# Two attention layers on one core: the first layer's head loop reordered, its value parts split in bulk, its low parts divided between VectorE and GpSimd

## What is computed

```python
text = ctx[:, :77]; ip = ctx[:, 77:]
q = split_heads(x @ Wq.T)
out_text = softmax(q @ k(text).T * 0.25) @ v(text)
out_ip   = softmax(q @ k_ip(ip).T * 0.25) @ v_ip(ip)
x = (out_text + out_ip) @ Wo.T + bo + x
```

## Time and profile before

| | |
|---|---|
| median of 3 runs | 1808.93 us (1806.72 to 1810.32) |
| the profiled execution's own time | 1810.82 us |
| its span | 1809.0 us |
| TensorE busy (matmul) | 1635.4 us, 90% |
| TensorE weight loads | 1234.2 us, 68% |
| VectorE busy | 1272.7 us, 70% |
| ScalarE busy | 1116.1 us, 62% |
| GpSimd busy | 463.6 us, 26% |
| mean granted clock | 0.96 |

### The profile page before, as it was taken

The page is one execution under the profiler, slowest core; times in us unless marked ns, Lnnn a source line. Parts: engine busy times, 40 slices in busy tenths (PEclk is TensorE's granted clock), DMA queues, the critical chain, the costliest instruction groups (busy, mean ns, idle before and its releaser), DMA issues.

```text
span 1809.0 us, 34075 instructions
## 1 busy us (share of the span) xinstructions
PE 1635.4 (90%) x8608; PEld 1234.2 (68%) x8608; DVE 1272.7 (70%) x3548; ACT 1116.1 (62%) x2323; POOL 463.6 (26%) x1225
## 2 busy tenths in 40 slices
PE   5788989999978898999988888999998889999993
PEld 2455469999445447999835544999974554799991
DVE  2487358887678717888758853788875883588875
ACT  1599157776279627777429943677734991577760
POOL 0244013232025302323104411222301540233220
PEclk9899989999989998999989999999998999899996
DMA  7210220000301031001030111100012102100000
GB/s 234 75 35 22 88 65 21 19 18 20 114 29 35 13 104 53 22 17 32 1 121 31 35 48 61 59 20 17 28 45 85 35 26 79 36 18 21 17 20 15
DMA packets 47284, 83.04 MB, mean 46 GB/s; under 512 B 4417, under 2 KB 11857, under 8 KB 47185
## 3 DMA queue, kind: packets, MB, share of 16 engines
q1 hardware_dynamic: 43040, 74.15, 12.5%
q10 hardware_dynamic: 4144, 7.76, 1.4%
HBM read 47.78 MB, written 34.10 MB: 45 GB/s over the span
## 4 chain that ended last, share of the span: by engine, by line
PE 77%; ACT 10%; issue 5%; DVE 5%; DMA 1%; POOL 1%; ACTq 1%; SPq 0%; POOLq 0%; DVEq 0%
PE ps_w L838 37%; PE ps_s L838 17%; PE ps_t L838 16%; PE ps_b L838 4%; ACT probsT_high L461 4%; ACT probsT L469 4%; DVE row_max L648 2%; PE ps_m L838 2%; ACT q_slot L454 1%; ACT probs L495 1%; POOL probsT_low L383 1%; ACT probs L478 0%; ACT probs L536 0%; DMA w_ki<-in_wki 0%; DVE row_max L679 0%
## 5 line engine op out<-in xcount | busy, mean ns | idle before, releaser
L637 DVE TENSOR_TENSOR probsT_low<-probsT,probsT_high 128x512 fp32r<-128x512 f32 x560 | 394.1, 704 | 85.2 <-ACT probsT L469 76.0
L461 ACT ACTIVATE probsT_high<-ps_t 128x512 fp32r<-128x512 f32 x640 | 382.6, 598 | 113.9 <-PE ps_t L838 109.9
L838 PE MATMUL ps_w<-gram,probsT_high 128*128 128x416 f32 (+2 forms) x1280 | 390.8, 316 | 0.0
L469 ACT ACTIVATE probsT<-ps_t 128x512 f32<-128x512 f32 x640 | 384.0, 600 | 0.0
L838 PE MATMUL ps_w<-gram_low,probsT_high 128*128 128x384 f32 (+2 forms) x1280 | 354.5, 305 | 0.0
L495 ACT ACTIVATE probs<-ps_s,exp_bias 128x508 f32<-128x508 f32 x320 | 220.9, 691 | 125.9 <-POOL exp_bias L394 82.6
L838 PE MATMUL ps_s<-k_slot,q_slot 96*128 96x512 f32 x640 | 249.6, 434 | 32.0 <-issue 13.0
L838 PE MATMUL ps_t<-q_slot,k_slot 98*128 98x512 f32 x640 | 266.1, 435 | 11.0 <-ACT q_slot L454 9.2
L394 POOL TENSOR_SCALAR exp_bias<-row_max 128x1 f32<-128x1 f32 x320 | 129.7, 405 | 551.8 <-DVE row_max L679 551.8
L838 PEld LDWEIGHTS ps_w<-gram_low,probsT_high 128*128 128x128 f32 (+1 forms) x1280 | 244.8, 191 | 11.1
L838 PEld LDWEIGHTS ps_w<-gram,probsT_high 128*128 128x128 f32 (+1 forms) x1280 | 243.2, 190 | 11.5
(11 more groups left out here) (153 smaller groups left out, 2056.9 us busy)
## 6 DMA issues: line engine op xcount, KB each, us to landing
q_slot<-parts_q SPq DMA_DIRECT2D x160, 96.0 KB
k_slot<-parts_k SPq DMA_DIRECT2D x160, 96.0 KB
parts_k<-probsT_high SPq DMA_DIRECT2D x24, 512.0 KB, 4.2
parts_q<-probsT_low SPq DMA_DIRECT2D x24, 512.0 KB, 4.3
parts_k<-probsT_high SPq DMA_DIRECT2D x24, 128.0 KB, 3.8
parts_q<-probsT_low SPq DMA_DIRECT2D x24, 128.0 KB, 3.6
ctx_sb<-in_ctxT ACTq DMA_DIRECT2D x3, 1024.0 KB, 8.3
vip_rep<-vip_rows SPq DMA_DIRECT2D x16, 160.0 KB, 3.6
```

The lines of the kernel that those rows point to most:

```text
L461: nc.scalar.activation(probsT_high[1 - par][:, t, :], ps_t[:, t % 2, :], ACT.Exp, scale=SCALE)
L469: nc.scalar.activation(probsT[:, t, :], ps_t[:, t % 2, :], ACT.Exp, scale=SCALE).then_inc(pt_block[l], 1)
L637: nc.vector.tensor_tensor(probsT_low[1 - par][:, t, :], probsT[:, t, :], probsT_high[1 - par][:, t, :].bitcast(F32), ALU.subtract).then_in ...
L838: return nc.tensor.matmul(out, lhsT, rhs, start=start, stop=stop)
```

## The change

In the first layer's head loop:
- **Order.** Scores are made three heads ahead instead of two (`AHEAD = 3`), through a loop of its own (`run_heads0`, 24 steps instead of 22). TensorE's order in a step is new; the transposed scores 0 of a head are the last work of the step before. The transposes of the outputs, their sum on VectorE and with it `out_all` come one step later.
- **Low parts.** Blocks 0 and 2 on GpSimd, 1 and 3 on VectorE, block 3 one step later.
- **Values.** Instead of four GpSimd operations per head that split the values, ScalarE writes the high parts and VectorE the low parts of all heads at once (`v0_high`, `v0_lows`), and GpSimd only copies both into the slot (two copies). The banks of these products are now freed by VectorE. `v0_lows` stands in the closing piece, behind the last of four groups of products.
- **Memory.** `v0_sb` becomes `v0_text` and `v0_ip`; `sz_all`, `fused`, `ip_sq`, `ip_norm2`, `rip` become parts of `out_all`; `ident` becomes `ident_r`.

```diff
 NEXT = (
     [("k0", m, "D") for m in range(CBN)]
     + [("q0", m, "D") for m in range(CBN)]
-    + [("v0t", 0, "A")]
-    + [("v0i", t, "A") for t in range(TB)]
+    + [("v0t", 0, "D")]
+    + [("v0i", t, "D") for t in range(TB)]
 )
...
+        def run_heads0(step, eng, b):
+            for n in range(-AHEAD, 1):
+                step(b, n, n % SLOTS, n // SLOTS, False, n >= 0, n >= -1, n >= -2, True)
+            with eng.Fori(0, TURNS - 1) as turn:
+                for n in range(1, SLOTS + 1):
+                    step(b, SLOTS * turn + n, n % SLOTS, turn + n // SLOTS, True, True, True, True, True)
+            for n in range(HEADS - AHEAD, HEADS + 1):
+                step(b, n, n % SLOTS, n // SLOTS, True, n < HEADS, n + 1 < HEADS, n + 2 < HEADS, False)
...
             # gpsimd
+                def low(t):
+                    pool.wait_ge(pt_block[0], TB * (g + 1) + t + 1 + CREDIT1)
+                    pool.sem_inc(passed, 1)
+                    nc.gpsimd.tensor_tensor(probsT_low[1 - par][:, t, :], probsT[:, t, :],
+                                            probsT_high[1 - par][:, t, :].bitcast(F32), ALU.subtract).then_inc(low_pool, 1)
+                if transposed:
+                    pool.wait_ge(oT_moved, g + CREDIT)
+                    pool.sem_inc(passed, 1)
+                    by_part = v0_slot[1 - par][:, :, :].rearrange("p t (g w) -> p t g w", w=V0H)
+                    nc.gpsimd.tensor_copy(by_part[:, :, 0:2, 0:D], v0_ip[:, :, n + 1, :, :])
+                    nc.gpsimd.tensor_copy(by_part[:, 0, 2:4, 0:D], v0_text[:, n + 1, :, :]).then_inc(v0_in, 1)
+                    low(0)
+                    low(2)
...
             # scalar
                 if transposed:
                     expT(b, 0, n, par, 0)
                     expT(b, 0, n, par, 1)
+                    expT(b, 0, n, par, 2)
+                if shifted:
+                    shift(b, 0, n + 1, k + 1)
+                if transposed:
+                    expT(b, 0, n, par, 3)
                 if use:
                     act.wait_ge(oT_done, HEADS * b + n + 1)
                     nc.scalar.activation(outT0[par], ps_w[par][0:V0S, :], ACT.Copy).then_inc(oT_moved, 1)
-                if transposed:
-                    expT(b, 0, n, par, 2)
-                if scores:
-                    shift(b, 0, n + 1, k + 1)
-                if transposed:
-                    expT(b, 0, n, par, 3)
...
             # vector
-            nc.vector.memset(v0_sb[:, :, :, :], 0.0)
...
+            def v0_lows(b):
+                before = 0 if b is FIRST else (1 + TB) * (b + 1)
+                def by_head(name, t, k):
+                    wait_job(dve, b, name, t)
+                    dve.wait_ge(v0_high_in, before + k + 1)
+                    return bank(name, t)[:, 0:C].rearrange("p (h d) -> p h d", d=D)
+                nc.vector.tensor_tensor(v0_text[0:TEXT0, :, 0, :], by_head("v0t", 0, 0)[0:TEXT0, :, :],
+                                        v0_text[0:TEXT0, :, 1, :].bitcast(F32), ALU.subtract).then_inc(freed["D"], 1)
+                for t in range(TB):
+                    nc.vector.scalar_tensor_tensor(out=v0_ip[:, t, :, 0, :], in0=by_head("v0i", t, 1 + t),
+                                                   scalar=ip_rows[:, 0:1] if t == 0 else 1.0,
+                                                   in1=v0_ip[:, t, :, 1, :].bitcast(F32),
+                                                   op0=ALU.mult, op1=ALU.subtract).then_inc(freed["D"], 1)
...
-                if scores:
-                    maxima(0)
-                if transposed:
-                    lowT(b, 0, n, par, 0)
-                if scores:
-                    maxima(1)
-                if transposed:
-                    lowT(b, 0, n, par, 1)
+                if use:
+                    lowT(b, 0, n - 1, 1 - par, 3)
+                if shifted:
+                    maxima(g + 2, row_max[0][par], 1)
+                if before:
+                    dve.wait_ge(o_done, g)
...
+                if transposed:
+                    lowT(b, 0, n, par, 1)
                 if scores:
+                    maxima(g + AHEAD, row_max[0][1 - par], 0)
...
                     if ahead and i < 2:
                         for m in ((0,), (1, 2))[i]:
                             low(b, "q0", m)
+                    if ahead and i == 3:
+                        v0_lows(b)
                     link(b, last)
...
             # tensor
+                if transposed:
+                    scoresT_of(0, g, k, 1)
+                if use:
+                    pe.wait_ge(oT_moved, g - 1 + CREDIT)
+                    pe.wait_ge(v0_in, g + 1)
+                    for t in range(TB):
+                        values_high(t)
+                if before:
...
+                    last.then_inc(o_done, 1)
+                if transposed:
+                    scoresT_of(0, g, k, 2)
+                if use:
+                    values_low(0)
+                    values_low(1)
+                if shifted:
+                    pe.wait_ge(max_half, 2 * (g + 3) + CREDIT)
+                    head_maxT(0, par)
+                if scores:
+                    scores_half(0)
+                if use:
+                    values_low(2)
+                    values_low(3).then_inc(oT_done, 1)
+                if transposed:
+                    scoresT_of(0, g, k, 3)
+                if scores:
+                    scores_half(1)
+                if shifted:
+                    scoresT_of(0, g + 1, k + 1, 0)
```

More of the change, by code:

```diff
@@ L572, in batch @@
                     highs(b, "q0")
[L573 to L575 removed]
+                    v0_high(b)
                 move_transposed(b, "tr1")
@@ L582, in _ @@
             highs(FIRST, "q0")
-            v0_text(FIRST)
-            for t in range(TB):
-                v0_ip(FIRST, t)
+            v0_high(FIRST)
             run_batches(act, batch)
@@ L638, in lowT, with step0, maxima @@
                                         ALU.subtract).then_inc(low_block[l], 1)
-            def step0(b, n, k, turn, use, transposed, scores):
+            def step0(b, n, k, turn, before, use, transposed, shifted, scores):
                 par = k % 2
-                def maxima(half):
+                g = HEADS * b + n
+                def maxima(j, rows, half):
                     cs = slice(2 * half, 2 * half + 2)
-                    dve.wait_ge(s_half, 2 * (HEADS * b + n + 2) + half + 1)
-                    nc.vector.tensor_reduce(out=row_max[0][par][:, cs, 0:1], in_=ps_s[:, :, 0:TEXT0], axis=AX.X, op=ALU.max)
-                    nc.vector.tensor_reduce(out=row_max[0][par][:, cs, SHIFT_ROWS - 1:SHIFT_ROWS], in_=ps_s[:, :, TEXT0:T],
+                    dve.wait_ge(s_half, 2 * j + half + 1)
+                    nc.vector.tensor_reduce(out=rows[:, cs, 0:1], in_=ps_s[:, :, 0:TEXT0], axis=AX.X, op=ALU.max)
+                    nc.vector.tensor_reduce(out=rows[:, cs, SHIFT_ROWS - 1:SHIFT_ROWS], in_=ps_s[:, :, TEXT0:T],
```

166 lines of the change are left out of this document (60 added, 106 removed).

## The result

The changed kernel takes **1821.57 us** (median of 5 runs, 1816.8 to 1822.75), the kernel before 1808.93 in the same comparison. The ratio is 1.0067, with a 95% interval of 1.0054 to 1.0081: slower by two thirds of a per cent. The profiled execution took 1822.75 with a span of 1820.9, 11.9 more than the span before (1809.0).

What follows compares the result with a forecast made beforehand. The prediction saw the first layer's head loop as a closed circle of waits, 5.46 us per head. Terms -9.8 (head stages), +10.6 (bulk split), +7.5 (clock), -0.8 (start) sum to +7.5: 1808.93 becomes 1816 us, range 1798 to 1825.

Steps and rivals of the forecast that it cites:

- The closing pieces: Last products to transposes: bulk value passes on VectorE delay the transposes by 3.55 us in three preparations, +10.6 us.
- The clock behind them: Output projections: TensorE's idle time drops its clock, costing 2.5 of a 3.05 us difference, three times, +7.5 us.
- rival 2: Closing pieces: the clock doesn't fall, as the last product splits the idle time; 1809 us, no change; chance 0.17.
- The first exponential: Fill of each head stage: transposed scores 0 of head 0 wait behind head 1's second score half, 2.45 us later.
- The steady head: First layer's head loop: the circle closes at 5.23 us instead of 5.46, 0.23 less per head, 3.9 for 17.
- I take 1.0 off: Fill of each stage: first two head spacings, no longer tied to the old circle, save 1.0 us (bounds 0 and 1.6).
- rival 3: Fill of each stage: low clock lasts one more head, 1.7 us times four, 6.8, giving 1823 us; chance 0.10.
- Rival 1: Head loop: VectorE and GpSimd don't hold each other up; ScalarE bounds heads at 5.06, about 1805 us; chance 0.20.
- the two readings: VectorE's lengthened subtraction: it stood still until GpSimd was done (chosen, head 5.23), or overlap costs a fixed 0.13 (5.11).
- the rule quoted in the prediction: VectorE instructions with two SBUF inputs and GpSimd instructions reading SBUF exclude each other for the whole instruction.
- 0.07 left over: Probability kept for what the prediction didn't see, split evenly; half was added to "faster", given as 0.27.
- The start's -0.8: Start of the kernel: VectorE's memset of 640 columns replaces one of 1600, so first loads wait 0.8 us less.

Runs made afterwards that it cites:

- e1: Changed kernel with the closing piece's five value-splitting passes spread: two behind the third product, one behind the fourth, two behind the last sum; 1803.92 us, ratio 0.9985.
- e2: Changed kernel with four unused matmuls added on TensorE ahead of the closing transposes in three preparations; 1812.69 us, ratio 1.0032.
- e3: Changed kernel without GpSimd's counting instruction between its wait for a block of exponentials and its subtraction; 1808.43 us, ratio 1.0023.
- e4: Changed kernel with GpSimd's block 0 subtraction replaced by four zero fills, so that low part is left out of the result; 1809.78 us, ratio 1.0017.
- e6: Changed kernel with an unused matmul ahead of each wait on a maximum while a stage's pipeline fills; 1811.18 us, ratio 1.0013.
- e7: Changed kernel with value passes spread, GpSimd's counting instruction removed, and VectorE's half 0 maximum and TensorE's first score half moved earlier; 1791.12 us, ratio 0.9910.
- e9: Changed kernel with spread value passes, no GpSimd counting instruction, earlier maximum and first score half, plus unused matmuls in the fill; 1789.67 us, ratio 0.9886.
- e5: Changed kernel with VectorE's half 0 maximum ahead of block 1's subtraction and TensorE's first score half directly behind transposed scores 2; 1804.93 us, ratio 0.9987.
- e8: Changed kernel with block 0's low part back on VectorE and GpSimd keeping block 2 alone; 1809.28 us, ratio 1.0016.

## Why the prediction was right or wrong

- **The closing pieces** were right in mechanism and size: 5.50 to 5.66 against 1.92, forecast +3.55 each. e1 and e2 show that the order of the passes makes it.
- **The clock behind them** was right: 2.8 instead of 2.5 each. Its price was read from the earlier trace rows as if that stretch were all at the low clock; in the trace the granted clock is 0.50 until 1798.68 and 1.00 after it, so the 3.05 are the price of 7.45 us at the low clock. The changed kernel's projections have 6.8 us of it, which is why the figure fitted. The prediction set rival 2 (no fall) at 0.17. In the changed kernel's profile all three fell, but e3 and e4 show that rival 2 isn't wrong in kind (below).
- **The first exponential** comes 9.82 after the first scores, before 7.37: the forecast 2.45.
- **The steady head failed by half.** The step was "GpSimd takes block 0 at once, as it does now". In the kernel before, GpSimd takes block 3 with a wait and the subtraction alone; block 0 is now taken in a helper with a counting instruction between. It starts 0.18 after the exponential, not 0.07, and as VectorE's end follows GpSimd's, the 0.11 passes into the circle: 5.36 instead of 5.23. e3 took the instruction out and got most heads back to 5.26. The prediction read "at once" from a row and didn't ask whether the new code issues the same instructions. Per head the gain was 0.13 (5.49 to 5.36, the loop's turns included), not 0.23, so 6.9 us of the forecast gain are missing over 68 heads.
- **"I take 1.0 off" in the fill failed**: nothing in the trace showed it, and it was not there. Taking 2.2 for the heads and 2.45 for the first exponential from the stage's +0.1 leaves -0.2. The first spacing between heads grew from 6.59 to 7.21 in the mean, since the clock stays low longer (in batch 2 until 18.6 us after the first scores, before until 14.3): rival 3, in part. e6 shows that the waits in the fill cost 1.2 per stage through it.
- **Rival 1 was priced wrong.** It gave a head of 5.06 if VectorE and GpSimd didn't touch each other. e4 took GpSimd's work away from beside VectorE's and got 5.24 to 5.27, since TensorE's own row closes at 5.24. Had rival 1 come true, the time would have been within 3 us of the forecast (5.24 to 5.27 per head against 5.23), not 12 below. Of the two readings the one that the prediction chose, that GpSimd's end sets VectorE's, is right. With four different starts the distance is the same:

| where | GpSimd's end | VectorE took | VectorE's end after it |
|---|---|---|---|
| before | 125.27 | 0.82 | 0.56 |
| changed | 126.53 | 1.01 | 0.54 |
| e3_direct | 126.18 | 0.91 | 0.55 |
| e7_joined | 132.46 | 1.33 | 0.55 |

The last pair in the joined run:

```profile
131.18 1.28 POOL L387 TENSOR_TENSOR probsT_low<-probsT,probsT_high 128x512 fp32r<-128x512 f32 x1 [0.64 <-ACT probsT L480]
...
131.68 1.33 DVE L657 TENSOR_TENSOR probsT_low<-probsT,probsT_high 128x512 fp32r<-128x512 f32 x1
```

A fixed price of 0.13 for an overlap can't give 1.33. The distance holds over whole traces: in the changed kernel, e3 and e7 all 84 of VectorE's subtractions that start during one of GpSimd's end 0.54 or 0.55 after it, and the 396 others take 0.68 to 0.69. These rows agree with the rule quoted in the prediction, of the Trainium skill's page "SBUF — State Buffer", section "Who interferes with whom". As 0.55 is less than the 0.69 of a subtraction alone, 0.14 of one is done before GpSimd's end; which part, no run tells.

- **Missed: the second layer**, 6.9 us shorter. Its head takes 10.25 instead of 10.29, which is 2.9 over 68 heads; of the other 4.0, 1.08 in each of batches 2 and 3 lies in the first spacing (12.6 to 11.5). No experiment was aimed at either. Every variant shows the 10.25 to 10.26, but the whole piece is anything from 2.3 (e9) to 10.6 us (e3) shorter than before, so the 6.9 belong to this execution. The cause is open.
- **Slips in the working.** With 0.07 left over and split evenly, "faster" comes to 0.235 and not 0.27. The upper bound of the head stages, 5.35 per head with a full fill, is +2.3 and not 0. Neither changes the forecast. The start's -0.8 came out at -1.07, but the first scores stand between 58.0 and 60.2 in the variants' profiles, so one profile doesn't confirm it.

## What to carry over

When the tightest circle of a pipeline is shortened, work out the next one too, engine by engine: here 5.36, 5.24 and another 5.24 lay close behind one another, and no order tried came near the gain of 0.4 per head that ScalarE's row would allow. Work that moves to another engine carries its own waits and bookkeeping instructions, and a latency read from a row holds for the instruction sequence of that row alone. Ahead of a stretch that TensorE bounds, put extra passes where other work covers them, since idle time there is paid once as waiting and, in 13 of 18 pieces measured, a second time by the clock.

## What was not expected of the hardware

**Behind the same idle time the clock sometimes falls and sometimes doesn't.** Six kernels have the closing piece as the change made it, the changed one itself, e3, e4, e5, e6 and e8, which makes 18 such pieces in the profiles, with the transposes 5.50 to 5.67 after the products and TensorE idle 2.6 to 2.8 us. The projections behind took 12.0 in 5 of them, 13.2 in 4, 14.8 in 8 and 16.4 in one. In the variants where the idle time was filled or gone (e1, e2, e7, e9) it was 12.0 in 12 of 12. Two pieces of e4, one behind an idle time that left the clock up, one behind one that didn't:

```profile
480.59 0.63 PE L1081 MATMUL ps_s<-ident_r,probsT 128*128 128x128 f32 x4 [2.64 <-DVE probsT L841]
```

```profile
483.00:486.00 3.00, 3.00 (x7) 1.00 (x7) 0.00 (x0) 0.00 (x0) 0.44 (x2) 1.00 0.20 76
```

```profile
1362.39 0.83 PE L1081 MATMUL ps_s<-ident_r,probsT 128*128 128x128 f32 x4 [2.63 <-DVE probsT L841]
```

```profile
1365.00:1368.00 3.00, 2.32 (x3) 1.18 (x4) 0.00 (x0) 0.55 (x1) 0.00 (x0) 0.50 0.19 74
```

The work ahead and the idle time (2.64 and 2.63) are the same in both, so neither decides alone; what does, the runs don't show. Of the 14 pieces with 2.63 or 2.64 five kept the full clock, of the four with 2.79 none. Two consequences follow. A variant that shifts such a piece can gain or lose up to 8 us without having changed it: of the 17.4 us between the spans of the changed kernel and e3, 6.0 are the heads', 5.6 two projections at full clock, and of the rest 3.7 lie in the second layers and 2.4 in the last batch's projection, which the edit doesn't touch either. And the five variants among them spread over 10 to 16 us from run to run (e6 1804 to 1820), where e1, e2 and e7, without the idle time, spread over 7 to 8. That is no more than a hint: the changed kernel's five runs spread over 6, the 31 of the kernel before over 9, e9's four over 12.

**A counting instruction between a wait and the work** costs GpSimd 0.10 us here (it starts 0.18 after the exponential, without the instruction 0.08), and where GpSimd is the last in the circle the whole of it is paid in every head.
